# Quantising without the exponent pass: a scaled absolute value, a bias addition that reads PSUM, and earlier weight maxima

## What is computed

```python
def fake_quant_nvfp4(t):            # blocks of 16 contiguous elements
    v = t.reshape(-1, 16)
    amax = jnp.max(jnp.abs(v), axis=-1, keepdims=True)
    scale = jnp.exp2(jnp.ceil(jnp.log2(jnp.maximum(amax, 1e-30) / 6.0)))
    u = v / scale
    idx = jnp.digitize(jnp.abs(u), mids)      # grid 0 .5 1 1.5 2 3 4 6
    return (jnp.sign(u) * grid[idx] * scale).reshape(t.shape)

x = x + conv3x3(fake_quant_nvfp4(_ln_c(x)), fake_quant_nvfp4(L0_conv_w))
t = _to_tokens(x)
t = t + ffn_top2_of_8(_ln_t(t))     # gate, W1, gelu, W2, weighted sum
return _from_tokens(t, x)
```

## Time and profile before

| | |
|---|---|
| median of 3 runs | 216.85 us (216.72 to 216.90) |
| the profiled execution | 217.73 us, of which 215.8 us lie between the first and last instruction (the span) |
| busy in the span | PE 183.6, DVE 146.8, POOL 124.9, ACT 116.6 us |
| quantising stage on DVE | from 19.09 us to about 52.8 us |
| first expert product weighted by a gate | 92.66 us |

### The profile page before, as it was taken

The page is one execution under the profiler, slowest core; times in us unless marked ns, Lnnn a source line. Parts: engine busy times, 40 slices in busy tenths (PEclk is TensorE's granted clock), DMA queues, the critical chain, the costliest instruction groups (busy, mean ns, idle before and its releaser), DMA issues.

```text
span 215.8 us, 3603 instructions
## 1 busy us (share of the span) xinstructions
PE 183.6 (85%) x958; PEld 71.8 (33%) x958; DVE 146.8 (68%) x459; ACT 116.6 (54%) x153; POOL 124.9 (58%) x117
## 2 busy tenths in 40 slices
PE   2966297877756397989999999999999999999990
PEld 2954134434556243422222222222222222222220
DVE  0899999999977996387484584684683683344352
ACT  2439713170078474449665665665666656656640
POOL 7697225767253251346766576566567557666763
PEclk9999859699978769999999999999999999999997
DMA  6940000000000038658479479299298198397101
GB/s 187 308 70 3 0 2 2 2 0 0 3 0 0 0 102 169 134 122 181 96 162 205 96 171 205 60 199 211 72 206 181 65 206 172 87 198 162 52 0 49
DMA packets 16316, 22.33 MB, mean 103 GB/s; under 512 B 2344, under 2 KB 8112, under 8 KB 16304
## 3 DMA queue, kind: packets, MB, share of 16 engines
q1 hardware_dynamic: 16144, 22.04, 45.4%
q10 hardware_dynamic: 160, 0.15, 0.2%
HBM read 19.82 MB, written 2.36 MB: 103 GB/s over the span
## 4 chain that ended last, share of the span: by engine, by line
PE 51%; DVE 27%; DMA 9%; issue 6%; ACT 3%; SPq 1%; DVEq 1%; POOLq 1%; POOL 1%; ACTq 0%
PE ps L1093 26%; PE ps L1078 24%; DMA gbc<-gate_rows 6%; DVE ssum L615 3%; DVE xn L702 3%; DVE xn L721 3%; DVE xn L627 3%; DMA cw<-in_conv_w 2%; DVE w_lo L675 2%; DVE y_sb L854 1%; DVE gbc L698 1%; ACT hl L490 1%; DVE topi L815 1%; DVE work L727 1%; ACT work L419 1%
## 5 line engine op out<-in xcount | busy, mean ns | idle before, releaser
L400 POOL TENSOR_TENSOR x<-x,y_sb 128x512 f32 (+1 forms) x63 | 80.1, 1271 | 52.2 <-DVE y_sb L854 51.4
L543 ACT ACTIVATE work<-ps,bias_sb,w_back 128x1024 f32<-128x1024 f32 x64 | 76.9, 1204 | 49.7 <-PE ps L1078 49.6
L854 DVE SCALAR_TENSOR_TENSOR y_sb<-ps,bias_sb,gbc 128x512 f32<-128x512 f32 x64 | 47.9, 750 | 53.2 <-PE ps L1093 42.9
L1093 PE MATMUL ps<-work,w_sb 128*64 128x512 f32 x256 | 68.8, 617 | 1.2 <-DVE y_sb L854 1.1
L1078 PE MATMUL ps<-xT,w_hi 128*128 (+1 forms) x128 | 39.6, 392 | 0.0
L1078 PE MATMUL ps<-xT,w_lo 128*128 (+1 forms) x128 | 39.0, 387 | 0.0
L993 PE MATMUL ps<-qpad,cw_bd 128*128 128x512 bf16 x72 | 21.6, 457 | 6.3 <-POOL qpad L355 6.3
L1093 PEld LDWEIGHTS ps<-work,w_sb 128*64 128x64 f32 x256 | 12.8, 135 | 29.0 <-issue 24.2
L1078 PEld LDWEIGHTS ps<-xT,w_hi 128*128 128x128 f16 x128 | 8.3, 100 | 41.7 <-issue 40.6
L355 POOL TENSOR_TENSOR qpad<-work,xn 128x512 bf16<-128x512 f32 (+1 forms) x8 | 10.5, 1310 | 15.9 <-DVE work L727 15.9
L379 POOL TENSOR_TENSOR hl<-xn,hl x8 | 9.2, 1155 | 15.9 <-DVE hl L777 9.0
(11 more groups left out here) (112 smaller groups left out, 182.7 us busy)
## 6 DMA issues: line engine op xcount, KB each, us to landing
gbc<-gate_rows SPq DMA_DIRECT2D x16, 768.0 KB, 10.6
gbc<-gate_rows SPq DMA_DIRECT2D x16, 256.0 KB, 3.9
x_sb<-in_x SPq DMA_DIRECT2D x8, 256.0 KB, 5.0
out<-x SPq DMA_DIRECT2D x8, 256.0 KB, 10.9
w_raw<-in_W SPq DMA_DIRECT2D x2, 256.0 KB, 5.8
w_sb<-in_W SPq DMA_DIRECT2D x1, 256.0 KB
gate_rows<-gateT SPq DMA_DIRECT2D x8, 32.0 KB, 2.0
cw<-in_conv_w ACTq DMA_DIRECT2D x2, 72.0 KB, 4.0
```

The lines of the kernel that those rows point to most:

```text
L400: pool.tensor_tensor(x2[:, ds(c * W, W)], x2[:, ds(c * W, W)], y_sb[:, u % H_RING, :], ALU.add).then_inc(added, 1)
L543: act.activation(h_sb[:, u % H_RING, :], bank(H + 2 * (u % 2), 2 * W), ACT.Gelu, bias=b1_sb[:, u:u + 1], scale=w_back[:, u:u + 1]).then_in ...
L854: dve.scalar_tensor_tensor(y_sb[:, u % H_RING, :], bank(Y + u % 2), b2_sb[:, u:u + 1], gbc[:, slot, u, :], ALU.add, ALU.mult).then_inc(wei ...
L1093: last = pe.matmul(ps[r * CH:(r + 1) * CH, (Y + u % 2) * W:(Y + u % 2 + 1) * W], w2_sb[:, u, :], h_sb[:, u % H_RING, r * W:(r + 1) * W], s ...
```

## The change

The mask of the exponent goes. ACT now stores the absolute value in `work` (`ACT.Abs`), and `magics` is computed from it with another constant. The sign is then no longer in `work`, so `bias` reads the value from the chunk's PSUM bank, where the transpose left it; the bank must keep it until then. So the small PSUM areas for the weights move from banks 0, 2 and 7 to banks 5, 6 and 7, and the transposes of chunks 5, 6 and 7 on PE move behind `convolve(0)` and `convolve(1)`, with ACT's copies of them behind the convolution weights. `weight_maxima` moves ahead of `block_maxima(0)`, `weight_exponents` and `weight_powers` move forward by several steps, and the hardware loops are written out.

```diff
-MAGIC = 1.5 * 2.0 ** 22
+MAGIC = 2.0 ** 22
...
-        CWT, BT = 0, 2 * W
-        WT, WB = (NCH - 1) * W, (NCH - 1) * W + 128
+        CWT = (NCH - 2) * W
+        BT = CWT + TAPS * CH
+        WT, WB = (NCH - 3) * W, (NCH - 3) * W + 128
...
             def take_v(c):
-                act.activation(work[:, ds(c * W, W)], bank(c), ACT.Copy).then_inc(v_ready, 1)
+                act.activation(work[:, ds(c * W, W)], bank(c), ACT.Abs).then_inc(v_ready, 1)
...
-            for c in range(3, NCH - 1):
+            for c in range(3, NCH - 3):
                 take_v(c)
...
+            take_v(NCH - 3)
+            take_v(NCH - 2)
             take_v(NCH - 1)
...
-            def exponents(c):
-                dve.tensor_scalar(xn[:, ds(c * W, W)].bitcast(i32), work[:, ds(c * W, W)].bitcast(i32), EXP_MASK, None,
-                                  ALU.bitwise_and).then_inc(exponent_ready, 1)
...
-                dve.scalar_tensor_tensor(m, m, MAGIC, smallest.to_broadcast([128, BLKS, BLK]),
+                dve.scalar_tensor_tensor(blk(xn[:, ds(c * W, W)]), blk(work[:, ds(c * W, W)]), MAGIC, smallest.to_broadcast([128, BLKS, BLK]),
                                          ALU.mult, ALU.max).then_inc(magic_ready, 1)
...
-                dve.tensor_tensor(work[:, ds(c * W, W)], work[:, ds(c * W, W)], xn[:, ds(c * W, W)],
+                dve.tensor_tensor(work[:, ds(c * W, W)], bank(c), xn[:, ds(c * W, W)],
                                   ALU.add).then_inc(biased_ready, 1)
...
+            weight_maxima()
+            block_maxima(0)
             conv_weights()
-            with dve.Fori(1, 3) as c:
-                quantise_step(c)
-            weight_maxima()
-            quantise_step(3)
-            dve.wait_ge(const_ready, 2)
-            weight_exponents()
-            with dve.Fori(4, 6) as c:
+            quantise_step(0)
+            weight_exponents()
+            quantise_step(1)
+            weight_powers()
+            for c in range(2, NCH):
                 quantise_step(c)
-            weight_powers()
...
             for c in range(NCH):
                 convolve(c)
                 if c >= 2:
                     center_x2(c - 2)
+                if c == 0:
+                    pe.wait_ge(w_inv_ready, 1)
+                    transpose_xn(NCH - 3)
+                    transpose_xn(NCH - 2)
                 if c == 1:
-                    turn_weight_maxima()
-                if c == 2:
-                    spread_weight_powers()
+                    transpose_xn(NCH - 1)
```

More of the change, by code:

```diff
@@ L454, in _ @@
             normalise(NCH - 1)
-            for c in range(3, NCH - 1):
+            for c in range(3, NCH - 3):
                 take_v(c)
             act.wait_ge(bT_ready, 1)
+            act.wait_ge(cwT_ready, 1)
             act.activation(bias_sb[:, :], ps[:, BT:BT + 2 * EXPERTS], ACT.Copy).then_inc(bias_ready, 1)
@@ L717, in magics @@
                 dve.wait_ge(block_magic, c + 1)
-                dve.wait_ge(exponent_ready, c + 1)
-                m = blk(xn[:, ds(c * W, W)])
+                dve.wait_ge(v_ready, c + 1)
                 smallest = bscale[:, ds(c, 1), :].rearrange("p z b -> p (z b)").unsqueeze(2)
-                dve.scalar_tensor_tensor(m, m, MAGIC, smallest.to_broadcast([128, BLKS, BLK]),
+                dve.scalar_tensor_tensor(blk(xn[:, ds(c * W, W)]), blk(work[:, ds(c * W, W)]), MAGIC, smallest.to_broadcast([128, BLKS, BLK]),
                                          ALU.mult, ALU.max).then_inc(magic_ready, 1)
@@ L726, in bias @@
                 dve.wait_ge(magic_ready, c + 1)
-                dve.tensor_tensor(work[:, ds(c * W, W)], work[:, ds(c * W, W)], xn[:, ds(c * W, W)],
+                dve.tensor_tensor(work[:, ds(c * W, W)], bank(c), xn[:, ds(c * W, W)],
                                   ALU.add).then_inc(biased_ready, 1)
[L731 to L737, removed]
             def quantise_step(c):
                 block_bounds(c)
-                bias(c - 1)
+                if c > 0:
+                    bias(c - 1)
                 block_magics(c)
-                block_maxima(c + 1)
+                if c < NCH - 1:
+                    block_maxima(c + 1)
                 magics(c)
-                exponents(c + 1)
+            weight_maxima()
+            block_maxima(0)
             conv_weights()
-            with dve.Fori(1, 3) as c:
-                quantise_step(c)
-            weight_maxima()
-            quantise_step(3)
-            dve.wait_ge(const_ready, 2)
-            weight_exponents()
-            with dve.Fori(4, 6) as c:
-                quantise_step(c)
-            weight_powers()
[L757 to L761, removed]
+            quantise_step(0)
[3 more added lines that the diff above has]
+            for c in range(2, NCH):
+                quantise_step(c)
             bias(NCH - 1)
@@ L967, in _ @@
             pe.wait_ge(const_ready, 5)
-            for c in range(XN_BY_DVE):
+            for c in range(NCH - 3):
                 transpose_xn(c)
+            pe.wait_ge(xn1_ready, XN_BY_DVE)
+            pe.wait_ge(w_amax_ready, 1)
+            pe.transpose(ps[0:EXPERTS + 1, WT:WT + 128], w_amax[:, :], identf[:, :]).then_inc(w_maxT_ready, 1)
             pe.wait_ge(b_in, 80)
-            pe.wait_ge(v_ready, BT // W + 1)
+            pe.wait_ge(xn1_late, 2)
             for k in range(2):
@@ L976, in _ @@
             last.then_inc(bT_ready, 1)
-            transpose_xn(NCH - 2)
             pe.wait_ge(cwx_ready, 1)
@@ L983, in _ @@
             last.then_inc(cwT_ready, 1)
-            transpose_xn(NCH - 1)
+            pe.wait_ge(w_diag_ready, 1)
+            pe.matmul(ps[:, WB:WB + EXPERTS + 1], ones_row[:, :], w_diag[:, :],
+                      start=True, stop=True).then_inc(w_spread, 1)
             pe.wait_ge(cwbd_ready, 2)
@@ L1004, in center_x2 @@
                 center_chunk(c, x2, cent2)
[L1006 to L1016, removed]
             for c in range(NCH):
```

1 line of the change is left out of this document (removed).

## The result

The changed kernel takes 211.46 us (median of 4 runs, 210.71 to 211.78) against 216.83 us. The ratio is 0.975, with an interval of 0.972 to 0.978: 5.4 us less, where 4.0 had been forecast. The forecast's own figure was 212.8, with 211.8 to 213.8 for its own mechanism and 210.9 to 215.0 for the whole range. A second series of the changed kernel on another chip gave 211.56 against 216.92, a ratio of 0.975 (0.974 to 0.976).

A forecast was written before the change was run, and what follows sets the result against it. It took the end to follow the DVE chain through the quantising stage, where POOL and DVE hold each other up, to the gates' broadcast. Minus 4.8 plus 0.8 gave minus 4.0 us: 216.85 becomes 212.8, range 210.9 to 215.0.

The forecast's parts named there:

- its own mechanism: Quantising stage: POOL holds DVE's small operations as it held the mask, bias runs free; 211.8 to 213.8 us, chance 0.50.
- rival (c): Small DVE operations not held by POOL, or DVE slips between; last bias near 44, 2 us more saved, 210.9, chance 0.17.
- three signs of being wrong: Chunk 0's copy past 38, low halves waiting for the high ones, or last bias ending before 46 or past 50.
- The mask: Eight DVE instructions dropped: 3.3 us saved if the wait only goes elsewhere, about 8 if it vanishes.
- The bias from PSUM: DVE's bias reading PSUM costs nothing; up to 0.95 us saved at the last bias, or it is held as before.
- The front: DVE's start of the stage, from 19.09: weight work moved, not new; first bias ends at 25.8.
- The moved transposes: PE's transposes behind the first convolutions delay ACT's copy of chunk 0 to 36.8 from 30.98; POOL waits from 33.3.
- The pace of POOL: From 36.8 POOL runs without a gap, 1.27 us each; last bias at 48.0 instead of 52.76, 4.8 us saved.
- Behind the stage: Low halves of the weights, after the last bias: one more wait for POOL, minus 0.2 saved elsewhere, 0.8 us given back.
- The step from the stage to the end: Stage savings reach the end, since nothing in the expert products can be weighed before the first gates' broadcast lands.
- Rival (b): PE's clock stays low through convolutions 1 to 3, up to 1.6 us more each; 214.2 us, chance 0.20.
- Rival (e): PE becomes the bound, its clock low for all convolutions, ending near 65.0; 218.1 us, chance 0.04.

The follow-up runs named there:

- e2: The changed kernel with the exponent mask put back behind each magics: 215.11 us against 216.95 for the kernel before, ratio 0.990.
- e1: The kernel before with the mask alone taken out, output not the reference's: 213.20 us against 216.95, ratio 0.982.
- e3: The changed kernel with the bias reading the absolute value in SBUF instead of PSUM, output not the reference's: 213.40 us, ratio 0.984 to the kernel before.
- e5: The kernel before with DVE's quantising loops written out and the weight maxima ahead of the first block maxima: 216.15 us against 217.13, ratio 0.995.
- e12: The changed kernel with ACT's copy of convolution 0 ahead of that of chunk 7, on one chip with the changed kernel: 212.43 us against its 211.56.
- e10: The changed kernel with 16 unused matmuls of 128 columns on PE ahead of the first convolution: 211.46 us, ratio 0.977 to the kernel before.
- e7: The changed kernel with POOL's five residuals cut from 512 columns to 16, output not the reference's: 207.80 us, ratio 0.958 to the kernel before.
- e8: The kernel before with POOL's residuals cut to 16 columns, output not the reference's: 211.93 us, ratio 0.976.
- e11: The changed kernel with the residual of chunks 0 to 4 moved from POOL to PE, all output kept: 209.49 us against 216.92 for the kernel before.
- e6: The changed kernel with ACT's copy of convolution 0 ahead of that of chunk 7, first series: 212.57 us, ratio 0.979 to the kernel before.
- e9: The changed kernel unedited, run again: 211.56 us (211.19 to 213.77); its profiled execution was the one of 213.77.

## Why the prediction was right, and what it missed

The time, 211.46, lies in the range, but 0.3 below the 211.8 to 213.8 that the forecast gave its own mechanism, and between that and the 210.9 of rival (c). The mechanism is the forecast's all the same: the small operations are held, the last bias ended at 47.42 and not near 44, the low halves did not wait for the high ones (ready at 44.18, needed at 48.52), and none of its three signs of being wrong came up. What was off were sizes, and they add up: the profile was to be 213.7 and was 210.71, 3.0 less. Of this 0.6 is the last bias, 1.5 the low halves, and 0.95 the late broadcast of the profile before. Against the medians 1.4 is left.

*The mask.* "If the wait only goes elsewhere" it was. 3.3 us of free time forecast, 3.6 and 3.75 measured (e2, e1). The wait moved to the small operation (1.24), as the earlier trace rows had suggested; rival (c) fell.

*The bias from PSUM.* Costed at nothing, and so it was: a median of 0.686, against 0.682 for the norm's multiplication in the earlier trace rows and 0.681 for the bias from SBUF in e3. The estimated 0.5 us more that followed from the Trainium skill's page "VectorE: DVE Perf Modes", section on the TRN2 errata, did not appear; at 512 fp32 columns with two inputs the measurement decides, and it shows no difference. What reading PSUM frees is worth at most about 1.9 (e3). The Trainium skill's page "SBUF — State Buffer", section on who interferes with whom, has it that a DVE instruction with at most one SBUF input does not contend with GpSimd, and the trace agrees: 0.68 beside a POOL operation against 1.64.

*The front.* Biases 0 to 3 were to end at 25.8, 29.1, 31.85 and 34.6, and ended at 25.54, 28.76, 31.44 and 34.13. Right, each a little early. Of the weight maxima the forecast said "moved, not new". That missed that the place matters for what is beside them (e5).

*The moved transposes, "this is what the change adds".* The mechanism was there, and POOL did wait, from 32.9 to 35.37. The size was off. The forecast took the two transposes at 1.3 and convolution 1 at 2.6; the clock rose earlier and they took 1.03 and 2.19, so the first residual was 1.4 earlier than 36.8. And it is not a cost: with the residual earlier the kernel is 0.9 slower (e12).

*The pace of POOL.* The last bias at 48.0 forecast, 47.42 measured. Right within 0.6.

*Behind the stage.* "0.8 given back." This is the term that was mis-sized. POOL's residual of chunk 4 began at 46.10, before the last bias, and only the subtraction fell on the low halves: 2.66 instead of 3.37, so 0.7 was gained instead of 0.8 lost, 1.5 us of difference. Part of it hangs on the same 1.4 us of the first residual, since POOL's ten operations follow it without a gap. The rest is that they were held less: the last subtraction ended at 49.05, 2.5 before the 51.6 of the forecast, while the last bias was only 0.6 early, since the last magics waited for q6 and not, as forecast, for r3.

*The step from the stage to the end.* The conclusion held one for one; the reason given did not. The wait for the broadcast was named as the place where nothing can go on, and it is a wait that mostly costs nothing.

Rival (b), the clock, did not come about: convolutions 1 to 3 took 2.19 to 2.20 each. A rise about 1 us later goes with 0.6 us at the last bias and 0.9 at the gate product (e10's profile). Rival (e) fell with it; it had a centring at four matmuls and up to 0.9 us, but the trace shows eight records in 1.05 at full clock (L935), so PE's end was put too early there.

## What to carry to other kernels

When an operation on DVE is longer than its kind, look at what POOL did in the same span: if it ended just after POOL's (0.04 us for the small operation at 38.34, 0.28 for the mask and 0.55 for the magics of the earlier trace rows), part of its busy time is a wait. Taking the operation out saved only its free time here, since the next operation of that sort inherited the wait. What helped too was taking work off the other side (e7, e8, e11), or moving one input to PSUM (e3). Filling an idle spell on the engine that is not the bound can be a loss (e6, e12). And the profile of one execution should be set against the median before its difference is believed.

## What the runs showed of the hardware that was not expected

- A scalar operation of 32 columns is held by POOL for as long as a large one: 1.24 to 1.25 us against 0.17.
- Two landings of the same gate broadcast in the same kernel: one let the third product start at 85.21, one took 13.86 us and let it start at 87.15, with the same instructions on DVE within 0.02 us ahead of it. Why the landing was later stays open.
- What the late landing cost was more than its delay: PE idled for 1.4 us, the granted clock then stood at 0.50 from 88.2 to 91.6, and of the 3.06 us 1.68 are two product groups at 1.84 and 1.83 instead of 1.01 and 0.98 (e9).
- The clock's rise around convolutions 0 and 1 moves by up to about 3 us between profiles with the same work on PE ahead of it (e3 against e6). 16 matmuls in PE's gap ahead of convolution 0 did not change the time (e10, 211.46 against 211.56).
